# Loads of a cross attention's keys divided between two DMA queues by unit in place of by partition quadrant

## What is computed

```python
x = x + xattn(layernorm(x), ctx)      # x: 8 x 64 x 2048, ctx: 8 x 1601 x 2048
x = x + attn(layernorm(x), w_q, w_k, w_v, w_o)
x = x + ffn(layernorm(x), A_w, B_w, Wq_w, keys)

def xattn(query, key):
    a = einsum('bqd,bkd->bqk', query, key)
    e = softmax(a, axis=-1)
    return einsum('bqk,bkd->bqd', e, key)
```

## Time and profile before

| | us |
|---|---|
| median of 3 runs | 1567.48 |
| lowest, highest | 1562.41, 1570.23 |
| profiled execution: its time | 1564.69 |
| its span, first to last instruction | 1562.9 |
| TensorE, matmul busy | 1460.9 (93%) |
| VectorE busy | 806.3 (52%) |
| ScalarE busy | 471.4 (30%) |
| GpSimd busy | 585.0 (37%) |

### The profile page before, as it was taken

One profiled execution on the slowest core, in us unless ns is written; L12 is line 12 of the kernel. 1 busy time (PEld: TensorE's weight loads), 2 busy tenths in 40 slices (PEclk: granted clock), 3 DMA queues, 4 the chain that ended last, 5 costly groups with the idle time before them and its releaser, 6 DMA issues.

```text
span 1562.9 us, 23951 instructions
## 1 busy us (share of the span) xinstructions
PE 1460.9 (93%) x9593; PEld 1034.2 (66%) x9593; DVE 806.3 (52%) x1151; ACT 471.4 (30%) x626; POOL 585.0 (37%) x250
## 2 busy tenths in 40 slices
PE   0999988988997899999999999999999999999999
PEld 0333333333333788888888888888888888878777
DVE  2686775875864502744554465455446430367333
ACT  1132332332333322333333323333324232232221
POOL 0030330330342143664663663654665644420000
PEclk9999999999998999999999999999999999999999
DMA  9777878878843252233332332332332352230123
GB/s 338 241 237 208 295 256 222 308 228 218 297 151 127 60 181 82 81 94 95 107 100 88 107 90 71 107 107 78 102 88 81 107 162 81 83 106 1 36 72 135
DMA packets 178637, 219.93 MB, mean 141 GB/s; under 512 B 5904, under 2 KB 104208, under 8 KB 175920
## 3 DMA queue, kind: packets, MB, share of 16 engines
q1 hardware_dynamic: 150912, 166.42, 34.2%
q10 hardware_dynamic: 27648, 52.44, 10.6%
HBM read 207.82 MB, written 10.49 MB: 140 GB/s over the span
## 4 chain that ended last, share of the span: by engine, by line
PE 79%; DVE 8%; DMA 6%; ACTq 3%; issue 2%; ACT 2%; SPq 0%; DVEq 0%
PE ps L763 15%; PE ps L765 15%; PE ps L764 15%; PE ps L699 9%; DMA xa_raw<-in_ctx 5%; PE ps L1803 5%; PE ps L1804 5%; PE ps L1805 5%; PE ps L651 4%; ACTq L317 3%; DVE xa_kt L547 3%; PE ps L1743 2%; PE ps L671 1%; PE ps L1896 1%; PE ps L1768 1%
## 5 line engine op out<-in xcount | busy, mean ns | idle before, releaser
L763 PE MATMUL ps<-h_hi,w_hi 128*128 128x512 f32 x800 | 315.6, 395 | 1.3 <-DVE h_lo L1459 1.1
L765 PE MATMUL ps<-h_hi,w_lo 128*128 128x512 f32 x800 | 311.8, 390 | 0.0
L764 PE MATMUL ps<-h_lo,w_hi 128*128 128x512 f32 x800 | 311.4, 389 | 0.0
L1191 POOL TENSOR_TENSOR w_lo<-raw,w_hi 128x2048 fp32r<-128x2048 f32 (+1 forms) x52 | 212.8, 4097 | 260.1 <-ACT w_hi L1256 219.3
L547 DVE STREAM_TRANSPOSE xa_kt<-xa_raw 128x832 f32<-128x832 f32 (+1 forms) x208 | 193.7, 995 | 116.7 <-PE ps L651 90.9
L501 POOL TENSOR_TENSOR xa_x<-xa_x,xa_tmp 64x512 f32<-64x512 f32 x88 | 110.9, 1284 | 350.7 <-ACT xa_tmp L422 346.7
L651 PE MATMUL ps<-xa_kt,xa_q_t 128*64 128x416 f32 (+2 forms) x1024 | 199.6, 530 | 20.7 <-DVE xa_kt L547 14.6
L699 PE MATMUL ps<-xa_raw,xa_e_t 32*64 32x512 f32 (+1 forms) x3264 | 184.0, 593 | 0.0
L1547 DVE TENSOR_TENSOR rows<-rows,ps 128x512 f32<-128x512 f32 x168 | 115.6, 688 | 116.1 <-PE ps L1805 116.1
L763 PEld LDWEIGHTS ps<-h_hi,w_hi 128*128 128x128 f32 x800 | 150.2, 188 | 36.4 <-issue 6.5
L765 PEld LDWEIGHTS ps<-h_hi,w_lo 128*128 128x128 f32 x800 | 150.2, 188 | 32.0
(11 more groups left out here) (216 smaller groups left out, 1872.8 us busy)
## 6 DMA issues: line engine op xcount, KB each, us to landing
raw<-in_L_attn_w_q SPq DMA_DIRECT2D x32, 1024.0 KB, 5.9
raw<-in_L_attn_w_o SPq DMA_DIRECT2D x30, 1024.0 KB, 5.0
xa_raw<-in_ctx SPq DMA_DIRECT2D x48, 384.0 KB, 6.3
xa_raw<-in_ctx ACTq DMA_DIRECT2D x16, 832.0 KB
xa_raw<-in_ctx SPq DMA_DIRECT2D x16, 832.0 KB
xa_raw<-in_ctx ACTq DMA_DIRECT2D x32, 384.0 KB, 8.2
xa_raw<-in_ctx ACTq DMA_DIRECT2D x16, 768.0 KB
xa_raw<-in_ctx SPq DMA_DIRECT2D x16, 768.0 KB
```

The lines of the kernel that those rows point to most:

```text
L763: pe.matmul(out, hi, mov_hi, start=first, stop=False)
L764: pe.matmul(out, hi, mov_lo, start=False, stop=False)
L765: return pe.matmul(out, lo, mov_hi, start=False, stop=last)
L1191: pool.tensor_tensor(w_lo[:, n % 2, part], raw[:, n % 2, part], w_hi[:, n % 2, part].bitcast(F32), ALU.subtract).then_inc(w_lo_done, 1)
```

## The change

A table of quadrants by queue becomes one by the kind of unit, and a unit's loads go to one queue: odd units to SyncE's (queue 0) in the order 0, 2, 1, 3, even units to ScalarE's (queue 1) in the order 2, 0, 3, 1.

```diff
-QUEUE_QUADS = ((0, 1), (2, 3))
+UNIT_QUADS = ((2, 0, 3, 1), (0, 2, 1, 3))
...
         at = UNIT * place(u)
-        for i in QUEUE_QUADS[queue]:
+        for i in UNIT_QUADS[u % SIDES] if queue == 1 - u % SIDES else ():
             for j0, j1 in piece_runs(u, g, i):
```

## The result

The changed kernel takes 1665.22 us (median of 4 runs, 1660.00 to 1666.78) against 1565.79 us for the kernel before in the same runs: a ratio of 1.0631, 95% interval 1.0602 to 1.0661, or some 99 us. The forecast was 1648 us, with a range of 1588 to 1690.

A forecast was written before the change was run, and what follows sets the result against it. Chain of waits: TensorE 79%, DMA 6%, ScalarE's sequencer 3%; the change touches only ctx loads in the cross attention. +20 +71 +1.7 +7.5 -16.4 = +83.8 on 1564.7 us gave 1648 us, range 1588 to 1690.

The forecast's parts named there:

- Start, +20: Before the first products with the values: ScalarE issues 38 blocks, not 31.5, often sharing one half's rate; +20 us.
- Urgent units late by 1.7 undisturbed: Stages' odd units of ctx: 13 blocks at 210 GB/s on SyncE's queue alone land 1.7 us late.
- The meeting, +4.1 and +3.4: ScalarE's whole unit, half the time on the urgent unit's half, delays it 4.1 us (13 blocks) or 3.4 us (12).
- turns: Rival, chance 0.20: whole unit starts only once the urgent one is through, all stage data at 210 GB/s; 1656 us.
- Stores, 3 x 2.5: In three stages a 1 MB store of x1 stands between SyncE's loads: 2.5 us each, 7.5 us.
- Waits that go, -16.4: In the stages: ScalarE's late half no longer matters for urgent units, so 16.4 us of earlier waits go.
- Issues at no cost: In the stages: ScalarE's 4 issues (6 or 8 before) and SyncE's additional ones cost nothing; evacuations under 1 us later.
- If the queue is full ... that cover still holds: ScalarE's evacuations in the stages: even if an issue takes several us, the 15 us until the next products cover it.
- ACTq no longer in the chain behind L370: Sign of being right: ScalarE's sequencer leaves the chain of waits after its table load (L370).
- queue limit: Rival, chance 0.17: the limit is the queue's for 2 KB rows, two queues make 379 GB/s anywhere; +32, 1597 us.
- Always on the same half: Rival, chance 0.10: the queues always meet on one half; start +38.5, +103 in all, 1706 us.
- Not slower: Rival, chance 0.08: one queue alternating halves keeps both busy, deciding from about 235 GB/s; urgent units in time, 1555 us.

The follow-up runs named there:

- whole_late: The changed kernel, but ScalarE issues its whole unit behind its evacuations in place of ahead of them: 1679.01 us, 1.0742 of the kernel before.
- thin_whole: The changed kernel, but ScalarE loads only the last block of every quadrant of even units from unit 6 on: 1613.51 us, 1.0293 of the kernel before.
- whole_order: The changed kernel, but ScalarE loads an even unit's quadrants as 0, 2, 1, 3 in place of 2, 0, 3, 1: 1660.28 us.
- same_half: The kernel before, with quadrants (0, 2) and (1, 3) for the two queues, so both begin on the same half: 1630.54 us, 1.0406.
- urgent_fine: The changed kernel, but SyncE's loads of odd units are cut to two blocks at most, going round quadrants 0, 2, 1, 3: 1716.65 us, 1.0945.

## Why the prediction was right, and where it was not

The sign, the range and the mechanism in the large held: loads by unit put each unit on one half at a time. Its sum of +83.8 stands against +102.0 in the profiled execution: 1.0 of the missing 18 lies in the start, 11.8 in the stages (63.8 forecast, 75.6 measured) and 5.3 behind them. Term by term:

- **Start, +20: +21.0.** V(0) went from 60.69 to 81.73, and putting the start back gave 20.7 by the medians. The table load, forecast near 54, came at 55.18. That the queues meet on one half half of the time gave the right size; 213 GB/s there and 377 elsewhere (42 to 46 us) are in the trace. "Nothing covers it" was right too. But the issues ahead of ScalarE's own work were the smaller part: with that work moved ahead in both kernels, V(0) still differs by 16.8 us.
- **Urgent units late by 1.7 undisturbed: 1.4 to 2.2.** `whole_late` has waits of 1.36 and 1.35 us for 12-block units that are through before ScalarE's rows move, `thin_whole` 2.16 and 2.24 with a few of these beside them. SyncE's queue was a little faster than forecast (228 GB/s for 210, perhaps because its neighbouring loads are on different halves), but in `thin_whole` its last rows were slow. The stages of `thin_whole` take 425.4 us, 11 more than the 414 that follow from the same terms without the whole unit: that is nearly all that is missing in the stages.
- **The meeting, +4.1 and +3.4: 3.8 on the mean.** 13 stages were to cost 13 x 3.75 = 48.8; the bytes of the whole units cost 49.6. That the size fits is luck, for the step behind it failed. I had the whole unit move from V+13, with 7.4 us (over 700 rows) of the urgent unit left, and the two queues share while on one half. In fact ScalarE's unit, issued at V+12, has its first row 3.8 to 6.2 us later, at V+15.7 to V+18.5. In the first four stages SyncE then has only 52 to 221 rows left, 0.5 to 2.2 us at 100 rows a us, but these take 5.0 to 6.5 us (4.2 to 5.7 in `whole_order`, with ScalarE on the other half); `whole_order`, built on my step, brought none of its 20 to 45 us. Only where SyncE is behind, by a store or by a whole unit still running (321 to 651 rows left), do the two share evenly for long, as from 232 to 238 us in the stage of V(4):

```profile
q10 hardware_dynamic: 379, 0.75, 55.1%
q1 hardware_dynamic: 381, 0.68, 50.0%
```

  What the runs showed in its place is nearest to the rival "turns", which had 1656 us: the two transfers stand mostly one behind the other, and from the first row of the urgent unit (V+4.1) to the last of the whole one they take 31.1 us in the first stage, which is 34.2 us long. But the rival had the urgent unit late by 1.7 alone and the next one held up. In the change that is so only at V(6) and V(10); in the plain stages the whole unit is through 1.0 to 3.9 us behind the next V, before the next urgent one moves (V+4.1), and the lateness is that of the slow last rows. In the first stages all these accounts give the same 32 to 34 us, which is why the total came out nearly right.
- **Stores, 3 x 2.5: 2.5.** In `thin_whole` the three stages with a store have the first transpose at V+25.3, 24.9 and 24.5, against 22.4: 2.9, 2.5 and 2.1 more. In the change the stages of V(6) and V(10), with no store of `x1`, wait 9.2 and 8.0 us, nearly as long as the three with one (9.0 to 9.8). Before V(6) SyncE issues a load of 1 MB of `x` at 261.84, ScalarE's issues are held up as told above, and the whole unit ends at 291.2, 7.7 us behind V(6); the urgent unit's first row comes at V+5.8. The rival "turns" had the transfers of `x` ("no longer hide"), my sum had not.
- **Waits that go, -16.4:** ScalarE's late half of an urgent unit is gone from the chain, as forecast.
- **Issues at no cost:** so it was in 12 of the 14 stages; in the first, ScalarE's evacuation ends at 99.4 us, and the next products begin at 115.9. From V(5) and V(9) it was not: there four issues last 8.6 and 8.2 us, the fourth alone 7.19 and 6.81 where the ones before it take 0.5, and the chain goes through them and L438 to the next V. "If the queue is full ... that cover still holds" was wrong for these, and so was the sign "ACTq no longer in the chain behind L370". The price is small, some 1 us each by an estimate: from the first transpose to the next V these stages take 9.1 and 8.4 us, the other second halves 7.6 to 8.3.
- **TensorE's clock in the stages, not in the sum:** about the end of the waits the granted clock falls to 0.50 for 3 to 10 us a stage, behind stretches in which TensorE was busy less than half the time (2.69 of 5.80 us from 100 to 105.8, 2.87 of 6.90 from 133 to 139.9); its mean is 0.86 to 0.95 in each of the first 13 stages (0.89 to 1.00 before). It explains little of the 75.6 us: in the stages of 13-block units the first transpose is followed by the next V after 8.1 to 8.6 us, against 8.1 before.
- **Not in the sum: +5.3 behind V(14).** Most of it seems to be TensorE's clock. The stretches 686 to 692.9 and 692.9 to 699.7 us of the change (window, busy times by engine, granted clock, DMA share, GB/s):

```profile
686.00:692.90 6.90, 6.13 (x38) 5.12 (x37) 0.00 (x0) 2.40 (x2) 0.63 (x2) 1.00 0.52 154
692.90:699.70 6.80, 6.80 (x24) 5.93 (x24) 3.67 (x3) 0.19 (x1) 4.01 (x1) 0.50 0.15 42
```

For 6.8 us the granted clock is 0.50 (1.2 GHz), then 1.00 again, with TensorE busy 6.13 of the 6.90 us before it; the kernel before has 1.00 at the same work. That costs 3.4 us by an estimate (6.8 us of work at half the clock). A second such stretch, 3.4 us from 1611.1, would cost 1.7 more, so that the two nearly make up the 5.3. Why the clock falls there was not tried.

The rival "queue limit" is out by `same_half` (215 GB/s for two queues). "Always on the same half" is out by 377 GB/s from 42 to 46 us. "Not slower" was to decide from about 235 GB/s for SyncE alone; it had 228 with the order as it is, so this was close in rate, and `urgent_fine` reached 256, but even then the whole unit, not the urgent unit's own rate, set the time.

## What to carry to other kernels

When loads are divided between two queues, divide them so that both queues are always on different halves of the partitions and the same unit ends on both at once: here 372 to 379 GB/s against 212 to 228. Giving each queue whole units puts each of them, and much of the time both together, at the rate of one half, and makes them stand mostly one behind the other; neither another order of the quadrants (`whole_order`) nor a later issue (`whole_late`) won that back here. Before dividing loads anew, look at what stands behind them in the issuing engine's program order: moving ScalarE's own work ahead of loads that are wanted later, and three times loads ahead of a normalization, gained 1.1% in the kernel before, and every new division tried lost.

## What the runs showed of the hardware that I had not expected

- A load issued on a second queue while the first is saturating one half has its first packet 4 to 6 us after the issue (93.67 to 99.83, 127.66 to 133.46 us), and 1.0 to 1.6 us after it when the first queue has nothing waiting (`whole_late` behind the urgent unit; `urgent_fine` in the stages without a store). Once it moves, the last rows of the first queue get a tenth of the engines (11.6% from 134 to 138.2 us); with 600 rows left the two share evenly. The first two look like engines that work off what they have already taken in before they turn to the other queue; that was not shown.
- In the tail of such a load, one row in some 28 is SyncE's, as if only one of the 16 engines still had rows of it. The trace doesn't name engines, so this stays open.
- A load whose outermost dimension is 4 ran on 4 of 16 DMA engines, at 102 GB/s, and the kernel that used it for whole units was 322 us slower than the change.
- A row of 2 KB takes 82 ns when unhindered; rows that wait for a half take about twice as long, and the engines show as 100% busy all the same, at 212 GB/s as at 379. A busy share of DMA near 100% says nothing about how near the transfer is to its best rate.
